# Projections: the normalized rows are stored as rows and turned by VectorE in 32x32 blocks in the query pass, not by TensorE in the key pass

## The reference

```
at = ctx_2048                        # (4, 1024, 1024)
hs = (x - mean(x)) / sqrt(var(x) + 1e-5)      # layernorm of each row, no gain
k = at @ Wk.T + bk;  v = at @ Wv.T + bv;  q = hs @ Wq.T + bq
... 16-head attention over k, v with a mask, output projection, layernorm, residual
... layernorm, router, top 8 of 64 experts (gate, up, silu, down), residual
```

## Time and profile before

| | us |
|---|---|
| median of three runs | 6763.86 (6763.16 to 6765.04) |
| the profiled execution: its time | 6763.85 |
| the profiled execution: its span, first to last instruction | 6762.0 |
| mean granted TensorE clock | 0.992 of full speed |
| TensorE matmul busy | 6614.3 (98%) |
| VectorE, ScalarE, GpSimd busy | 3302.4 (49%), 2933.3 (43%), 1147.4 (17%) |
| first matmul; first of V; first of Q; last of Q | 12.90; 392.58; 741.76; 1089.70 |
| first matmul of the attention | 1106.43 |

### The profile page before, as it was taken

The page is one execution under the profiler, slowest core; times in us unless marked ns, Lnnn a source line. Parts: engine busy times, 40 slices in busy tenths (PEclk is TensorE's granted clock), DMA queues, the critical chain, the costliest instruction groups (busy, mean ns, idle before and its releaser), DMA issues.

```text
span 6762.0 us, 107799 instructions
## 1 busy us (share of the span) xinstructions
PE 6614.3 (98%) x34530; PEld 5884.0 (87%) x34531; DVE 3302.4 (49%) x4252; ACT 2933.3 (43%) x3606; POOL 1147.4 (17%) x1015
## 2 busy tenths in 40 slices
PE   9999998999999999699999999999999999999998
PEld 7888887887888788599989999999999999999998
DVE  4443324999999899732443334322422323323333
ACT  3321224888888644432443334322422333333333
POOL 1000000000000155511211211111111212111121
PEclk9999999999999999899999999999999999999999
DMA  8853555555555666455676566654644556556555
GB/s 257 231 197 143 155 143 145 129 127 128 128 129 128 182 171 171 128 156 130 178 211 172 152 174 189 160 137 106 186 106 106 134 134 162 148 147 162 155 153 152
DMA packets 733960, 1048.19 MB, mean 155 GB/s; under 512 B 301281, under 2 KB 531425, under 8 KB 733858
## 3 DMA queue, kind: packets, MB, share of 16 engines
q0 software_dynamic: 109792, 368.12, 23.5%
q1 hardware_dynamic: 467680, 381.55, 22.1%
q10 hardware_dynamic: 156386, 297.29, 13.0%
HBM read 724.43 MB, written 322.31 MB: 155 GB/s over the span
## 4 chain that ended last, share of the span: by engine, by line
PE 51%; DMA 4%; issue 1%; ACT 1%; DVE 1%; ACTq 0%; SPq 0%; POOLq 0%; DVEq 0%
PE moe_ps_y L1332 5%; PE moe_ps_gate L1345 5%; PE moe_ps_gate L1346 5%; PE moe_ps_gate L1347 5%; PE moe_ps_up L1347 5%; PE moe_ps_up L1346 5%; PE moe_ps_up L1345 5%; PE moe_ps_y L1334 5%; PE moe_ps_y L1333 5%; DMA out<-moe_y,moe_rec_s 2%; PE moe_ps_xT L1322 2%; PE moe_ps_hT L1353 1%; DMA moe_rec_s<-table 1%; DMA first_raw<-in_w_up 1%; ACT moe_gu_hi L1375 0%
## 5 line engine op out<-in xcount | busy, mean ns | idle before, releaser
L1449 DVE SCALAR_TENSOR_TENSOR moe_hidden<-moe_silu,moe_rec_w,moe_ps_up 128x384 f32<-128x384 f32 x286 | 175.8, 615 | 1384.6 <-PE moe_ps_up L1347 1190.3
L1345 PE MATMUL moe_ps_gate<-moe_gu_hi,moe_xT_hi 128*128 128x384 f32 x2288 | 793.4, 347 | 11.1 <-DVE moe_xT_lo L1442 7.5
L1300 POOL DMA_INDIRECT out<-moe_y,moe_rec_s x287 | 478.2, 1666 | 1909.9 <-DMA moe_rec_s<-table 1037.5
L1346 PE MATMUL moe_ps_gate<-moe_gu_lo,moe_xT_hi 128*128 128x384 f32 x2288 | 768.1, 336 | 0.0
L1347 PE MATMUL moe_ps_gate<-moe_gu_hi,moe_xT_lo 128*128 128x384 f32 x2288 | 767.8, 336 | 0.0
L1347 PE MATMUL moe_ps_up<-moe_gu_hi,moe_xT_lo 128*128 128x384 f32 x2288 | 765.1, 334 | 0.0
L1345 PE MATMUL moe_ps_up<-moe_gu_hi,moe_xT_hi 128*128 128x384 f32 x2288 | 764.2, 334 | 0.0
L1346 PE MATMUL moe_ps_up<-moe_gu_lo,moe_xT_hi 128*128 128x384 f32 x2288 | 764.2, 334 | 0.0
L1332 PE MATMUL moe_ps_y<-moe_d_hi,moe_hT_hi 128*128 128x512 f32 x1722 | 696.5, 404 | 3.0 <-DVE moe_hT_lo L1455 3.0
L1334 PE MATMUL moe_ps_y<-moe_d_hi,moe_hT_lo 128*128 128x512 f32 x1722 | 677.2, 393 | 0.0
L1333 PE MATMUL moe_ps_y<-moe_d_lo,moe_hT_hi 128*128 128x512 f32 x1722 | 669.6, 389 | 0.0
(11 more groups left out here) (202 smaller groups left out, 13975.2 us busy)
## 6 DMA issues: line engine op xcount, KB each, us to landing
first_raw<-in_w_gate ACTq DMA_DIRECT2D x63, 1536.0 KB, 9.6
first_raw<-in_w_up ACTq DMA_DIRECT2D x63, 1536.0 KB, 14.7
moe_raw_d<-in_w_down ACTq DMA_DIRECT2D x63, 1536.0 KB, 7.1
proj_a_raw<-in_ctxT POOLq DMA_DIRECT2D x64, 512.0 KB, 5.1
kst<-proj_o SPq DMA_DIRECT2D x256, 128.0 KB, 2.7
vst<-proj_o SPq DMA_DIRECT2D x64, 512.0 KB, 2.6
qst<-proj_o SPq DMA_DIRECT2D x256, 128.0 KB, 2.2
att_kt<-kst SPq DMA_DIRECT2D x64, 512.0 KB, 3.6
```

Of the source, the lines that this page charges most:

```text
L1300: nc.gpsimd.indirect_dma_start(out=acc[:, :], out_offset=bass.IndirectOffsetOnAxis(ap=rec_s[:].bitcast(I32)[:, 0:1], axis=0), in_=y[:], in ...
L1345: nc.tensor.matmul(o[:, 0:I], xT_hi[:, c], gu_hi[:, b, k, c], start=(c == 0), stop=False)
L1346: nc.tensor.matmul(o[:, 0:I], xT_hi[:, c], gu_lo[:, b, k, c], start=False, stop=False)
```

## The change

Nothing is transposed in the K pass. Each normalized tile is stored at once as rows of 4 KB to a scratch tensor `xnst` (4096 rows x 1024), with a row's features reordered on the way: the 1024 features are 8 chunks of 4 quarters of 32, and `xn` is written by quarter first. The Q pass loads, for every block, a quarter at a time: four DMAs (L198 of the new kernel), each to 32 of the 128 partitions of a tile `xg`, in runs of 256 elements (1 KB). `xg` lies over `xin` and `xn`, which are free by then. VectorE turns `xg` into `a_raw` by four STREAM_TRANSPOSE instructions of 128x1024 per block (L347), which transpose 32x32 blocks, and the splitting of Q into `a_hi` and `a_lo` now reads and writes with a rearranged access pattern. Identity matrix, `tps`, `xT` and its copies are gone. `G` (rounds) is now called `ROUNDS`.

```
+        rows = s.sb("rows", [P, 4, H])
+        xin, xn = rows[:, 0:2], rows[:, 2:4]
+        xg = rows[:].rearrange("p q n -> p (q n)").rearrange("p (g n) -> p g n", g=GROUPS)
-        acc, tps = s.ps("acc", [P, BANKS, HALF]), s.ps("tps", [P, 2, C, P])
+        acc = s.ps("acc", [P, BANKS, HALF])
...            POOL, loads
+                    if p == Q:
+                        if not is_first(t2, b):
+                            pool.wait_ge(turned_done, PIECES * t)
+                        for k in range(P // W):
+                            part = xnst[bass.ds(t * HALF, HALF), k * (H * W // P):(k + 1) * (H * W // P)]
+                            pool.dma_start(xg[k * W:(k + 1) * W], part.rearrange("(g b) n -> b g n", b=W)).then_inc(xg_in, 16)
+                        return
...            SyncE, K pass, even rounds
+                            sp.dma_start(xnst[bass.ds(j * P, P), :], xn[:, jb]).then_inc(xn_stored[jb], 16)
-                            sp.wait_ge(xT_done, j + 1)
-                            sp.dma_start(xnT_v[:, :, bass.ds(j * P, P)], xT[:, jb]).then_inc(xT_stored[jb], 16)
...            ScalarE
+                        act.wait_ge(turned_done, (2 * t2 + b) * PIECES + k + 1)
+                    nc.scalar.copy(split(p, a_hi, b, k), turned(p, k)).then_inc(a_hi_done, 1)
-                    nc.scalar.copy(xT[:, jb], tps[:, jb]).then_inc(xT_done, 1)
...            VectorE
+                def turn(p, t2, b, k):
+                    n = number(p, t2, b)
+                    dve.wait_ge(xg_in, 16 * (P // W) * (2 * t2 + b + 1))
+                    dve.wait_ge(a_lo_done, (n - 1) * PIECES + k + 1)
+                    columns_of_piece = slice(k * CP * W, (k + 1) * CP * W)
+                    nc.vector.transpose(a_raw[:, chunks(k)].rearrange("p c t -> p (c t)"), xg[:, :, columns_of_piece]).then_inc(turned_done, 1)
...
+                    nc.vector.tensor_scalar(by_quarter(xn[:, jb]), in_chunks(xin[:, jb]), mv[:, jb, 0:1], rstd[:, jb],
...
+                        if after and after[0] == Q and g < PIECES:
+                            turn(*after, g)
                         evacuate(p, t2, b, g)
...            TensorE
-                            for c in range(C):
-                                last = nc.tensor.transpose(tps[:, jb, c], xn[:, jb, c * P:(c + 1) * P], ident[:])
-                            last.then_inc(t_done, 1)
```

More of the change, by code:

```diff
@@ L28 @@
 TOPK = 8
+W = 32
+G = P // W
 REGION = 4096
@@ L61, in f32, with in_chunks, by_quarter, projections_pass @@
     return ap.bitcast(F32)
+def in_chunks(rows):
+    return rows.rearrange("p (j s a) -> p j s a", s=G, a=W)
+def by_quarter(rows):
+    return rows.rearrange("p (s j a) -> p j s a", s=G, a=W)
 def row_broadcast(dram_row, n):
     return dram_row.broadcast_to([P, n])
-def projections_pass(nc, ctxT, x, wkT, wvT, wqT, bk, bv, bq, xnT, kst, vst, qst):
+def projections_pass(nc, ctxT, x, wkT, wvT, wqT, bk, bv, bq, xnst, kst, vst, qst):
     H, T = ctxT.shape
@@ L102, in projections_pass @@
         dve_passed, sp_passed = s.sem("dve_passed"), s.sem("sp_passed")
-        sources = [src.rearrange("(c p) t -> p c t", p=P) for src in (ctxT, ctxT, xnT)]
-        xnT_v = sources[Q]
+        ctx_v = ctxT.rearrange("(c p) t -> p c t", p=P)
         weights = (wkT, wvT, wqT)
@@ L134, in stores_before @@
         def stores_before(p, t2, b, g):
-            return 16 * (sum(STORES[i] * NB * G // 2 for i in range(p)) + STORES[p] * ((2 * t2 + b) * (G // 2) + g // 2))
+            return 16 * (sum(STORES[i] * NB * ROUNDS // 2 for i in range(p)) + STORES[p] * ((2 * t2 + b) * (ROUNDS // 2) + g // 2))
         def piece(p, half, k):
@@ L151, in norm_tile, with turned, split @@
             return LN * (2 * t2 + b) + g // 2 if g % 2 == 0 else None
[L153 to L163, removed]
+        def turned(p, k):
+            raw = a_raw[:, chunks(k)]
+            if p < Q:
+                return raw
+            return raw.rearrange("p c t -> p (c t)").rearrange("p (g c b) -> p c g b", g=GROUPS, b=W)
+        def split(p, tile, b, k):
+            piece = tile[:, b, chunks(k)]
+            if p < Q:
+                return piece
+            return piece.rearrange("p c (g b) -> p c g b", b=W)
         def chunks(k):
@@ L179, in load @@
                             pool.wait_ge(a_lo_done, (n - 1) * PIECES + k + 1)
-                        pool.dma_start(a_raw[:, chunks(k)], sources[p][:, chunks(k), bass.ds(t * HALF, HALF)]).then_inc(a_in[k], 16)
+                        pool.dma_start(a_raw[:, chunks(k)], ctx_v[:, chunks(k), bass.ds(t * HALF, HALF)]).then_inc(a_in[k], 16)
                 load(K, 0, 0)
[L183 to L186, removed]
                 for dst, src in ((bias_k, bk), (bias_q, bq), (bias_v, row_broadcast(bv, H))):
@@ L268, in high @@
                     n = number(p, t2, b)
-                    act.wait_ge(a_in[k], 16 * (n + 1))
-                    nc.scalar.copy(a_hi[:, b, chunks(k)], a_raw[:, chunks(k)]).then_inc(a_hi_done, 1)
+                    if p < Q:
+                        act.wait_ge(a_in[k], 16 * (n + 1))
+                    else:
+                        act.wait_ge(turned_done, (2 * t2 + b) * PIECES + k + 1)
+                    nc.scalar.copy(split(p, a_hi, b, k), turned(p, k)).then_inc(a_hi_done, 1)
                 def evacuate(p, t2, b, g):
-                    n, q = number(p, t2, b) * G + g, g % 2
+                    n, q = number(p, t2, b) * ROUNDS + g, g % 2
                     if not (p == K and is_first(t2, b) and g < 2):
@@ L304, in body @@
                         weights_high(p, 1, 1)
-                    for g in range(G):
+                    for g in range(ROUNDS):
                         evacuate(p, t2, b, g)
@@ L1483, in scratch @@
         return nc.dram_tensor(name, shape, dt, kind="Internal").ap()
-    xnT = scratch("xnT", (H, T))
+    xnst = scratch("xnst", (T, H))
     kst, qst, vst = scratch("kst", (B * NH, 2 * HD, S)), scratch("qst", (B * NH, 2, HD, S)), scratch("vst", (T, NH, 2 * HD))
@@ L1489, in cross_attention_and_experts @@
     I = w_gate.shape[2]
-    projections_pass(nc, ctxT, x, wkT, wvT, wqT, bk, bv, bq, xnT, kst, vst, qst)
+    projections_pass(nc, ctxT, x, wkT, wvT, wqT, bk, bv, bq, xnst, kst, vst, qst)
     with ExitStack() as first_st:
```

58 lines of the change are left out of this document (20 added, 38 removed).

## The result

The changed kernel takes 6732.12 us (median of five runs, 6728.41 to 6733.36) against 6765.04 before in the same series; ratio 0.995, 95% interval 0.9936 to 0.9965. A second series of both gave 6732.91 against 6762.26, ratio 0.9955 (0.9941 to 0.9968), which is 6733.4 on the same footing and inside the range. The change is faster by half a percent, clear of the noise and in the direction forecast; the gain came out at 32.9 and 29.4 us where 29.1 stood.

A forecast was written before the change was run, and what follows sets the result against it. The prediction took TensorE's instruction issue to bound the projection passes. From 6763.85 us it subtracted 29.1 for the transposes and took everything added as free, giving 6734.8, with a range of 6732 to 6743 us.

The forecast's parts named there:

- Price of the transposes on TensorE, 29.1 us: K and V passes: removing 256 transposes saves 28.1 us in K and 1.0 in V, priced from distances between matmul starts.
- The busy time (69.6): Rival for K and V: the transposes cost TensorE their whole busy time, 69.6 us, giving 6694; no separate chance.
- Added cost nothing: VectorE: four block transposes per block, 1.2 us each, and the reordered accesses hide in idle time, at no cost.
- Transfers of K: K pass: DMA share at most 0.88, so hidden; the rival, K held by transfers, gave 6762.8, chance 0.03.
- stores landing in 2 to 4 us: K pass: claimed landing time of stores, used against the rival that K is held by its transfers.
- Loads of Q, upper bound 39.4 us: Q pass: a block's loads take at most 39.4 us at fixed packet cost; late-load rival 6744, chance 0.07.
- the tightest place: Second block of Q: load wanted 15 us after issue, 31 us of cover; at the upper bound about 9 us lost once.
- The limit of 8.2 us per turn and the 16 us of cover: Q: a block transpose fills VectorE only at 8.2 us; four banks cover late evacuations for 16 us. Slow-turns rival: chance 0.03.
- the terms put at nothing: Whole kernel: work added on VectorE and DMA queues costs nothing, and the 1.85 us between span and time stay.
- 1 or 2 us: Allowed shift of the restart in K, the barrier and the 16.7 us behind it, used for the forecast's width.
- The base of the sum, 6763.85: Time before the change from the profiled execution, from which the forecast subtracted 29.1 us.
- more than 31 us won: Whole kernel: case of a gain larger than the forecast range allows, given chance 0.02.

## Why the forecast came out 4.8 us high

- **Price of the transposes on TensorE, 29.1 us:** right. K and V lost 28.98 in the first trace and between 28.9 and 29.1 in every trace in which VectorE did not hold TensorE up in V. The busy time (69.6) would have missed, and so would the 390 ns that the Trainium skill (VectorE: DVE Perf Modes, The three transpose paths) gives for one in bf16 on TensorE: 28.98 / 256 is 0.113 us.
- **Added cost nothing:** right for the changed kernel (Q 347.93). The turn was put at 1.2 and took 1.24 us.
- **Transfers of K:** right. 0.81, below the 0.88 allowed. Only "stores landing in 2 to 4 us" was read too narrowly: those of L237 took from 2.2 to 9.3 us in the trace of before.
- **Loads of Q, upper bound 39.4 us:** wrong in its working. It took a packet for a run; the row had 3242 packets for 11.77 MB, 3.6 KB each, and not 2 KB. What did grow is the share per MB: 22.5% for 12.58 MB in 270 us instead of 13.7% for 11.77, 1.5 times. All four quarters landed 5.4 to 16.3 us after their issue, and the tightest place was the one named, the second block of Q: there stands the only turn that waited, 1.7 us.
- **The limit of 8.2 us per turn and the 16 us of cover:** wrong. The sum of VectorE's work over a block is no bound when its lag falls into four rounds and a burst of loads, released by the last turn, then makes ScalarE wait up to 12 us for a store. That wait was not in the forecast. The change itself has no lag, since its turns run in idle time of VectorE; one of about 3 us (3.7 us per turn) still fitted, and a turn of 5.8 us made the kernel slower than before. With turns of 1.24 us the wrong limit cost the forecast nothing.
- **The step that failed for the time: the terms put at nothing, and the width given to them.** The sum took only the transposes off. It left the restart, the handover to the attention and the stages behind as they were, and gave all of them "1 or 2 us", with three runs that spread 1.9 us for support. In the two traces they were 1.05 + 0.34 + 1.1 us, all in one direction. The base of the sum, 6763.85, lay another 1.2 us below the median of its own series (6765.04), and the gap between span and time shrank by 0.2. These 3.9 us and the 28.98 make the 32.9 of the first series. 59 runs of the kernel before lie between 6756.05 and 6767.01, mean 6762.7; 10 of the changed one between 6728.41 and 6734.33, mean 6732.0. The restart moved by 1.3 us (19.11 to 20.43) and the stages behind the projections by 6.4 us (5649.8 to 5656.2) among the twelve traces that compute the same there. A range of 5 us below the forecast would have been needed, and 2.8 were given. The chance of 0.02 for "more than 31 us won" was too small for the same reason: in seven comparisons with the kernel before in the same series (the changed kernel twice, and five variants with its passes) the means differ by 28.9 to 33.6 us.
- **Luck:** which side of the range's edge the result fell on. The first series put the result outside by 2.0 us, the second would have put it inside.
- **Open:** where the 1.7 us beyond 29.0 come from. The difference of the means above is 30.7, of which 29.0 is the change; 32 runs of the changed kernel and of the five variants with its passes have the same mean, 6732.0. By the spread of the single runs (2.2 and 1.9 us) that difference is good to about 0.4 us, an estimate that takes the runs of a series as independent, so the 1.7 are probably not scatter of the runs alone. Both traces of before have late restarts (20.4) and long rests (5655.6, 5656.2); others of the changed passes have 19.1 to 20.2 and 5649.8 to 5655.7. Two traces don't settle it; the identity is excluded.

## What to carry to other kernels

Price what leaves a saturated TensorE by the distance between starts in a pass with it and a pass without it; it was right to 0.12 us here, where busy time said 2.4 times as much. Count cover where the new work stands, with what it releases: work that is free in the sum over a block can use up most of the banks' cover in four rounds, and a burst of loads behind it takes the rest through the stores. Once TensorE stalled here, the cost was more than its waits, since the granted clock fell too (0.97 and 0.86 over the Q pass). Don't set a range of 2 us from three runs of a 6.8 ms kernel.

## What the runs showed that was not expected

STREAM_TRANSPOSE of 128x1024 fp32 took 1.24 us, as much as a two-operand subtraction of that size (1.225). Rearranging the write of `xn` in runs of 32 elements cost nothing (0.813 us). Loads in runs of 1 KB, 512 and 256 bytes took 22.5, 21.3 and 20.6% of the DMA engines for the same bytes, and halving the packets of K's queue (43601 to 21614, in 282 and 255 us) left its share at 63%, with 8% more bytes per us (49.78 and 48.70 MB). Behind a stall of 2.29 us TensorE ran at half its pace from 866.98 to 869.97 us, and with two extra transposes per turn the slower pace made 18.4 of the 58.0 us lost. 16 loads of 128 KB, issued over 10.3 us, delayed no store, where four of 512 KB in 2.6 us made ScalarE wait up to 7.8 us; both kernels take the same time.
